# A block-scheduled transformer kernel: the first layer's normalisations and two quaternion sums, done otherwise

## What is computed

```
xn = layernorm(x)                                    # n0
a  = linear attention of xn: elu(q)+1, elu(k)+1, kv = k^T v, num / (den + 1e-6)
y  = layernorm(xn + a) * g1 + b1                     # n1 (division by den: "at")
f  = y + (silu(y Wg + bg) * (y Wu + bu)) Wd + bd     # H0 = 341 hidden
x  = x + layernorm(f) * g2 + b2                      # n2
       + sum over 8 experts e of (silu(xn Wg_e) * (xn Wu_e)) Wd_e
xn = layernorm(x)                                    # n3
for l in 4 layers:                                   # on z = xn
    z = z + filter(hamilton(hamilton(Q(q), Q(k)), Q(v))) @ pw + pb   # q,k,v of layernorm(z): "A"
    z = z + gelu(layernorm(z) @ fw + fb) @ mw + mb                   # "C"
out = x + z + top-2 of 8 experts of xn
```

## Time and profile before

| | |
|---|---|
| median of 3 runs | 1518.19 us (1517.88, 1518.19, 1524.01) |
| the profiled execution | 1522.51 us |
| its span, first to last instruction | 1520.7 us |
| mean granted TensorE clock | 0.978 of full speed |
| TensorE, VectorE, ScalarE, GpSimd busy | 92%, 82%, 69%, 24% of the span |
| TensorE weight loads | 65% |
| memory traffic | 185.59 MB read, 43.86 MB written |

### The profile page before, as it was taken

How to read it: one execution, slowest core, us unless ns; L and a number is a source line. 1 busy time by engine, 2 the same in 40 slices (tenths; PEclk the granted TensorE clock), 3 DMA queues, 4 the chain that set the end, 5 groups by cost and what they waited for, 6 DMA issues and landing times.

```text
span 1520.7 us, 20946 instructions
## 1 busy us (share of the span) xinstructions
PE 1404.2 (92%) x6198; PEld 994.6 (65%) x6198; DVE 1253.9 (82%) x1575; ACT 1046.8 (69%) x2413; POOL 361.5 (24%) x251
## 2 busy tenths in 40 slices
PE   6999998999999999899998899999889999999876
PEld 4767765666666666566655667656667787777653
DVE  3443467876999989999959897999899998999995
ACT  6556557666886777766887767777767686776552
POOL 0001202310131412111131410130524343543410
PEclk9999999999999999999999899999999999999989
DMA  7754455244545554534263335455546465655262
GB/s 268 264 210 150 148 176 193 70 130 138 187 144 154 165 174 138 188 116 120 96 220 119 103 106 159 127 153 163 161 148 211 129 204 176 199 169 155 68 177 83
DMA packets 111244, 238.03 MB, mean 157 GB/s; under 512 B 13207, under 2 KB 52844, under 8 KB 109644
## 3 DMA queue, kind: packets, MB, share of 16 engines
q1 hardware_dynamic: 106588, 227.31, 48.2%
q0 software_dynamic: 4544, 9.38, 1.8%
HBM read 185.59 MB, written 43.86 MB: 151 GB/s over the span
## 4 chain that ended last, share of the span: by engine, by line
PE 37%; issue 24%; DVE 16%; ACT 10%; POOL 9%; DMA 3%; SPq 0%; POOLq 0%; ACTq 0%; DVEq 0%
PE bank L1353 7%; PE bank L1341 6%; PE bank L1343 6%; PE bank L1342 6%; POOL RSTD L1016 4%; POOL ytok L1031 4%; PE bank L1530 3%; ACT ROWS L856 2%; DVE SH L1207 2%; DVE AM L1075 2%; DVE TA L1071 2%; PE bank L1448 2%; ACT ROWS L869 2%; DVE AM L1079 1%; PE bank L1442 1%
## 5 line engine op out<-in xcount | busy, mean ns | idle before, releaser
L1016 POOL TENSOR_TENSOR RSTD<-SS,power_half 128x4 f32<-128x4 f32 x96 | 156.8, 1633 | 835.3 <-ACT ROWS L856 835.2
L1353 PE MATMUL bank<-SH,WD 128*128 128x512 f32 x512 | 262.8, 595 | 2.1 <-DMA WD<-in_w_d 1.6
L1341 PE MATMUL bank<-NH,GU 128*128 128x512 f32 x512 | 246.4, 481 | 0.5 <-DVE SH L1207 0.5
L1207 DVE TENSOR_TENSOR SH<-SH,bank 128x512 f32<-128x512 f32 x256 | 172.5, 682 | 88.0 <-ACT SH L844 48.8
L1071 DVE TENSOR_TENSOR TA<-QKV 128x2048 f32<-128x2048 f32 x96 | 219.6, 2287 | 1.3
L1343 PE MATMUL bank<-NL,GU 128*128 128x512 f32 x512 | 202.3, 395 | 0.0
L1342 PE MATMUL bank<-NH,GU 128*128 128x512 f32 x512 | 202.2, 395 | 0.0
L844 ACT ACTIVATE SH<-bank 128x512 f32<-128x512 f32 x256 | 153.4, 605 | 63.8 <-PE bank L1343 61.8
L1031 POOL DMA_INDIRECT ytok<-YS,XR x78 | 118.1, 1514 | 152.2 <-ACT YS L1004 138.1
L1075 DVE TENSOR_TENSOR AM<-AM,TA 128x1024 f32<-128x1024 f32 x128 | 153.2, 1217 | 0.5
L869 ACT ACTIVATE ROWS<-bank,RSTD 128x128 f32<-128x128 f32 x384 | 109.9, 373 | 56.5 <-POOL RSTD L1016 48.6
(11 more groups left out here) (234 smaller groups left out, 2858.1 us busy)
## 6 DMA issues: line engine op xcount, KB each, us to landing
GU<-halves SPq DMA_DIRECT2D x112, 512.0 KB, 4.4
QKV<-QKV SPq DMA_DIRECT2D x32, 720.0 KB
GU<-in_w_gu SPq DMA_DIRECT2D x39, 512.0 KB
xg<-in_c_fill SPq DMA_DIRECT2D x8, 2080.0 KB
WD<-in_w_d SPq DMA_DIRECT2D x128, 128.0 KB
FC<-ready_w SPq DMA_DIRECT2D x32, 512.0 KB
WQ<-ready_w SPq DMA_DIRECT2D x32, 384.0 KB
WD<-in_w_d SPq DMA_DIRECT2D x39, 256.0 KB
```

The lines of the kernel that those rows point to most:

```text
L1016: pool.tensor_tensor(RSTD[:], SS[:], (power_one if k[0] == "at" else power_half)[:], ALU.pow).then_inc(power_done, 1)
L1207: dve.tensor_tensor(SH[:, g % 4, :], SH[:, g % 4, :], banks[2 + g % 2][:], ALU.mult).then_inc(h_ready, 1)
L1341: pe.matmul(out, w_hi, x_hi, start=True, stop=False)
L1353: pe.matmul(banks[4][:], WD1[:, slot, :], SH[:, g % 4, :], start=first, stop=last).then_inc(down_done, 1)
```

## The change

Two parts of the program change, and with them the plan.

1. n0 to n3 are done as A and C are: TensorE transposes, VectorE sums the rows and makes SHIFT, ScalarE squares with it as bias. Nothing downstream takes the mean out there, so there is one more step, `offset`: after `power`, VectorE makes OFFSET = -SUMS/128 x RSTD, and ScalarE scales with Identity, bias OFFSET and scale RSTD. "at", A and C scale as before.
2. The last four single-slice sums of the quaternion product become two sums over pairs of slices; the second operand of each is read with a negative step (slices 2, 0 and 3, 1), for which `pair` learns to run backwards. `HAM` is 11 in place of 13.
3. The planned steps follow this, and every number in `TUNE` is another.

```diff
-HAM, FOLD = 13, 2
+HAM, FOLD = 11, 2
...
-                     "mlp_add", "mult", "split", "route", "table", "centre"),
+                     "mlp_add", "mult", "split", "route", "table", "centre", "offset"),
...
-    "early": 169.23,
-    "norm0": (-117.36, -300.1),
-    "keys": (153.9, 106.13),
+    "early": 96.43,
+    "norm0": (-125.46, -33.96),
+    "keys": (-264.35, -414.22),
...
-    "late": 189.14,
-    "pace": 1.09,
-    "prep": (-605.23, -390.98, 38.11, -347.49),
+    "late": 446.57,
+    "pace": 2.51,
+    "prep": (-329.52, 606.46, -124.49, 268.98),
...
-            if kind in ("A", "C"):
-                step("centre", k, urgency, [(PE, 0.44, ("LN",), gives), (DVE, 0.72), (ACT_, 1.37)], after)
-            else:
-                step("centre", k, urgency, [(PE, 0.89, ("LN",), gives), (ACT_, 1.37)], after)
+            step("centre", k, urgency, [(PE, 0.44, ("LN",), gives), (DVE, 0.79), (ACT_, 1.37)], after)
             step("power", k, urgency, [(POOL, 1.5)], [("centre", k, ACT_)])
-            step("scale", k, urgency, [(ACT_, 2.0 if kind == "n3" else 1.0, ("YF",) if kind == "n3" else ())], [("power", k, POOL, 0.06)])
+            ready = [("power", k, POOL, 0.06)]
+            if kind not in ("A", "C"):
+                step("offset", k, urgency, [(DVE, 0.1)], [("power", k, POOL, 0.1)])
+                ready = [("offset", k, DVE, 0.15)]
+            step("scale", k, urgency, [(ACT_, 2.0 if kind == "n3" else 1.0, ("YF",) if kind == "n3" else ())], ready)
...
-    token_means = [x for x in scalings if x[0] in ("A", "C")]
+    token_means = [x for x in scalings if x[0] != "at"]
...
-                if k in mean_no:
-                    act.wait_ge(shift_set, mean_no[k])
+                act.wait_ge(shift_set, mean_no[k])
...
+                if k[0] in ("n0", "n1", "n2", "n3"):
+                    act.wait_ge(offset_set, upto("offset", k))
                 for i in range(GROUPS):
-                    ins = act.activation(dst[:, i, 0:P], LNB[:, i * P:(i + 1) * P], ACT.Copy, scale=RSTD[:, i:i + 1])
+                    if k[0] in ("at", "A", "C"):
+                        ins = act.activation(dst[:, i, 0:P], LNB[:, i * P:(i + 1) * P], ACT.Copy, scale=RSTD[:, i:i + 1])
+                    else:
+                        ins = act.activation(dst[:, i, 0:P], LNB[:, i * P:(i + 1) * P], ACT.Identity, bias=OFFSET[:, i:i + 1],
+                                             scale=RSTD[:, i:i + 1])
...
         def pair(ap, a, b):
+            if a > b:
+                return ap[:, a:None if b == 0 else b - 1:b - a, :]
             return ap[:, a:b + 1:b - a, :]
...
-                    5: ((2, 3), (0, 1), ADD), 6: ((0, 1), (2, 3), SUB)}
+                    5: ((2, 3), (0, 1), ADD), 6: ((0, 1), (2, 3), SUB),
+                    8: ((1, 3), (2, 0), ADD), 9: ((0, 2), (3, 1), SUB)}
...
-            elif i < 12:
-                dve.wait_ge(ham, base + 8)
-                d, s, op = ((3, 0, ADD), (2, 1, SUB), (1, 2, ADD), (0, 3, SUB))[i - 8]
-                ins = dve.tensor_tensor(AM[:, d, :], AM[:, d, :], TA[:, s, :], op)
             else:
-                dve.wait_ge(ham, base + 12)
+                dve.wait_ge(ham, base + 10)
...
+            elif name == "offset":
+                dve.wait_ge(power_done, upto("power", k))
+                dve.wait_ge(rows_scaled, upto("power", k) - 1)
+                dve.scalar_tensor_tensor(OFFSET[:], SUMS[:], -1.0 / P, RSTD[:], ALU.mult, ALU.mult).then_inc(offset_set, 1)
...
-                        if k in mean_no:
-                            mm = pe.transpose(LNB[:, i * P:(i + 1) * P], src[:, i * P:(i + 1) * P], ident[:])
-                        else:
-                            mm = pe.matmul(LNB[:, i * P:(i + 1) * P], src[:, i * P:(i + 1) * P], centre[:], start=True, stop=True)
+                        mm = pe.transpose(LNB[:, i * P:(i + 1) * P], src[:, i * P:(i + 1) * P], ident[:])
```

More of the change, by code:

```diff
@@ L145, in run @@
                 spare.remove(min(spare))
-            elif name == "ham" and key[2] == 12:
+            elif name == "ham" and key[2] == HAM - 1:
                 spare.append((at + length + 0.2, self.half[key[0:2]]))
@@ L161 @@
 TUNE = {
-    "early": 169.23,
-    "norm0": (-117.36, -300.1),
-    "keys": (153.9, 106.13),
[L165 to L176, removed]
-    "late": 189.14,
-    "pace": 1.09,
-    "prep": (-605.23, -390.98, 38.11, -347.49),
+    "early": 96.43,
+    "norm0": (-125.46, -33.96),
+    "keys": (-264.35, -414.22),
+    "kv_sum": 10.07,
+    "query": (75.18, -842.28),
+    "attn": (37.84, -213.99),
+    "norm1": (-325.66, 130.32),
+    "ffn2": (112.18, -398.42),
+    "norm2": (436.81, -400.09),
+    "route": (-147.96, 161.64),
+    "norm3": (-539.34, -168.94),
+    "start": (19.69, -8.13),
+    "layer": -33.39,
+    "each": (129.08, 164.43, 7.76, -363.31, 70.0, 158.85, -393.03, -4.03, -111.96, 224.33, -155.01, 123.2, 49.89, -176.86, 135.18, -371.38, -316.27, 16.88, 211.37, 37.35, -122.3, -37.79, 78.26, -18.71, -212.2, -225.41, -350.08, 248.52, -857.21, 138.92, 161.32, -3.96),
+    "tile": (-128.54, -313.85, -266.06, -6.81, 19.88, 152.73, -402.05, 142.08),
+    "late": 446.57,
+    "pace": 2.51,
+    "prep": (-329.52, 606.46, -124.49, 268.98),
 }
@@ L329, in schedule @@
                      [("ham", (t, l, i - 1), DVE, 0.0)] if i else [("cosines", key, ACT_), ("differences", key, DVE), ("roll", key, SP, 5.0)])
-            step("fold", key, u + 1.2, [(DVE, 1.86, ("XG",), ("AM",))], [("ham", (t, l, 12), DVE, 0.0)])
+            step("fold", key, u + 1.2, [(DVE, 1.86, ("XG",), ("AM",))], [("ham", (t, l, HAM - 1), DVE, 0.0)])
             step("freq", key, u + 1.3, [(PE, 0.86, ("6",))], [("fold", key, DVE)])
@@ L427, in program @@
     SS, RSTD = sb("SS", [P, GROUPS]), sb("RSTD", [P, GROUPS])
-    SUMS, SHIFT = sb("SUMS", [P, GROUPS]), sb("SHIFT", [P, GROUPS])
+    SUMS, SHIFT, OFFSET = (sb(n, [P, GROUPS]) for n in ("SUMS", "SHIFT", "OFFSET"))
     ROWS = sb("ROWS", [P, GROUPS, P])
@@ L851, in _ @@
                 act.wait_ge(power_done, n)
-                if k in mean_no:
-                    act.wait_ge(shift_set, mean_no[k])
+                act.wait_ge(shift_set, mean_no[k])
                 for i in range(GROUPS):
-                    shift = SHIFT[:, i:i + 1] if k in mean_no else root_eps[:]
-                    ins = act.activation(ROWS[:, i, :], LNB[:, i * P:(i + 1) * P], ACT.Square, bias=shift, scale=P ** -0.5,
+                    ins = act.activation(ROWS[:, i, :], LNB[:, i * P:(i + 1) * P], ACT.Square, bias=SHIFT[:, i:i + 1], scale=P ** -0.5,
                                          accum_out=SS[:, i:i + 1])
@@ L867, in _ @@
                 act.wait_ge(turned_back, n)
+                if k[0] in ("n0", "n1", "n2", "n3"):
+                    act.wait_ge(offset_set, upto("offset", k))
                 for i in range(GROUPS):
-                    ins = act.activation(dst[:, i, 0:P], LNB[:, i * P:(i + 1) * P], ACT.Copy, scale=RSTD[:, i:i + 1])
+                    if k[0] in ("at", "A", "C"):
[3 more added lines that the diff above has]
+                                             scale=RSTD[:, i:i + 1])
                     if k[0] == "n3":
-                        ins = act.activation(SEND[:, i, 0:P], LNB[:, i * P:(i + 1) * P], ACT.Copy, scale=RSTD[:, i:i + 1])
+                        ins = act.activation(SEND[:, i, 0:P], LNB[:, i * P:(i + 1) * P], ACT.Identity, bias=OFFSET[:, i:i + 1],
+                                             scale=RSTD[:, i:i + 1])
                 ins.then_inc(rows_scaled, 1)
@@ L1072, in hamilton @@
             elif i in sums:
-                dve.wait_ge(ham, base + (2 if i < 4 else 5))
+                dve.wait_ge(ham, base + (2 if i < 4 else 5 if i < 7 else 8))
                 d, s, op = sums[i]
                 ins = dve.tensor_tensor(pair(AM, *d), pair(AM, *d), pair(TA, *s), op)
-            elif i < 12:
-                dve.wait_ge(ham, base + 8)
-                d, s, op = ((3, 0, ADD), (2, 1, SUB), (1, 2, ADD), (0, 3, SUB))[i - 8]
-                ins = dve.tensor_tensor(AM[:, d, :], AM[:, d, :], TA[:, s, :], op)
             else:
-                dve.wait_ge(ham, base + 12)
+                dve.wait_ge(ham, base + 10)
                 ins = dve.tensor_tensor(TA[:], AM[:], own(QKV[:, h, 2, :, :]), ALU.mult)
```

4 lines of the change are left out of this document (2 added, 2 removed).

## The result

The changed kernel takes **1563.2 us** (median of 4 runs, 1558.7 to 1564.1), the kernel before, in the same session, 1521.0 (4 runs, 1517.9 to 1524.0). The ratio is 1.027, with an interval of 1.0244 to 1.0296: 42 us slower, where 5 us faster were predicted. It lies outside the range of 1492 to 1538.

The account below looks back on a forecast made before the run. Neither TensorE nor VectorE alone was taken as the bound (weights 0.70 and 0.30 where both are full). TensorE -12.0, VectorE +4.1 and longer rounds +3.0 gave -4.9 us, from 1518.2 to 1513 us; range 1492 to 1538.

Parts of the forecast that it names:

- ScalarE's waits for SHIFT: ScalarE's squares in 32 more normalisations wait for SHIFT: some 32 us more lost, of engine time not the bound.
- the 10 to 16 that were to show the prediction right: Sign on TensorE: its busy time was to fall by 10 to 16 us if the prediction was right.
- The order: All five engine queues reordered by the new TUNE: taken as 0, with 15 us kept on both sides.
- The round itself: Longer n0 to n3 normalisations: 0.5 us beyond what is counted, on 6 of 18 rounds, +3.0 us.
- TensorE's saving: Transposes replace centring products in 32 normalisations: 14.4 us of work saved, priced at -12.0 us.
- Rival 1: TensorE is the bound all through, its 14.4 us come whole: about 1502 us; chance 0.36 together with better orders.
- Rival 2: VectorE is the bound from 380 us on, so its added work counts: 1535 us; chance 0.17.
- theory W: Forecast for e8 that VectorE's added work sets the cost: +5 to +15 us.
- Rival 3: Bank 5, through which normalisations go one at a time, becomes the bound: 1526 to 1565 us; chance 0.10 beyond 1525.8.

Follow-up runs that it names:

- e1: Kernel before in its own queues, with only the last four quaternion sums made two large ones with a backward operand: ratio 0.997, 1521.1 us.
- e4: Work of the kernel before (centring products, four single-slice sums) in the changed kernel's queues: 1.0235 of the kernel before, 1561.1 us.
- e17: Work of the kernel before in the changed kernel's sequence of tiles and layers, interleaving found by local search: 1.0052 of the kernel before.
- e2: Kernel before in its old queues, only n0 to n3 done the new way, VectorE's new steps inserted at the old plan's times: 1.0467, 1597.4 us.
- e7: Kernel before in its own order, n0 to n3 using transposes with the mean left in, no row sums, SHIFT or OFFSET: ratio 0.9974.
- e8: Kernel before in its own order, n0 to n3 with transposes, row sums and SHIFT, but no OFFSET and Copy scalings: 1.0259, 1557.2 us.
- e16: Changed kernel's work in the kernel before's sequence of tiles and layers, interleaving found by local search: 1.0177 of the kernel before, 1544 us.
- e3: All of the new work, n0 to n3 and large sums, in the queues of the kernel before: ratio 1.0479, 1597.7 us.
- e10: Changed kernel with other urgency offsets, 319 of its 3921 steps moved over 3 places: 1.0293 of the kernel before, 1566.1 us.
- e11: Changed kernel with one urgency offset changed (attn, -256.38 for -213.99), 232 steps moved: 1.0295 of the kernel before, 1567.6 us.
- e13: Changed kernel's work in its own sequence of tiles and layers, interleaving found by local search: 1.0269 of the kernel before.
- e5: Changed kernel with each 2080 KB fill sent as pieces, one behind each expert weight load: 1.0185 of the kernel before, 0.85% under the changed kernel.
- e6: Kernel before with each 2080 KB fill sent as 8 pieces, one per visit: ratio 0.9924.
- e15: Kernel before's work in its own sequence, interleaving found by local search, plus two large backward-operand sums and fills in pieces: 1.0042 of the kernel before.

## Why the prediction was wrong

**What was right.** The prices of single operations, nearly all. The transposes take 0.60 us a group. OFFSET takes 0.155 us, with 0.17 taken. The scalings with a bias take 0.46. The 192 large sums, backward operand or not, take 1217 ns, at most 1249, as the 128 of before did: a negative step cost nothing here. e1 gained 4.6 us by the ratio, with an interval from 1 to 8; the prediction had 4.7 us of VectorE work, priced at 1.4. VectorE's busy time rose by 27.5 us (25 to 30 predicted). ScalarE's waits for SHIFT rose from 64.2 to 87.4 us (32 more predicted). TensorE's work did shrink by about 14: against e4, in the same order and at nearly the same granted clock (0.969 and 0.968), it is busy 13.0 us less. But its busy time against the kernel before fell by 1.5 us and not by the 10 to 16 that were to show the prediction right.

**The step that failed first: "*The order*", taken as 0 with 15 us either way.** Measured with the old work it was +36 us (e4). I treated the order as luck, independent of the work, and had no row for its size. The lengths that the planner was given changed with the work. By the planned lengths, from `centre` to `turn`, a round of n0 to n3 went from 0.89 + 0.2 + 1.37 + 0.2 + 1.5 + 0.06 + 1.0 + 0.2 = 5.42 us to 0.44 + 0.2 + 0.79 + 0.2 + 1.37 + 0.2 + 1.5 + 0.1 + 0.1 + 0.15 + 1.0 + 0.2 = 6.25. That was to be read from the diff: 32 x 0.83 = 27 us of longer rounds. In the plan itself, worked out with each kernel's `schedule()`, the time from the start of `centre` to the start of `turn` on TensorE went from 6.7 to 8.7 us, with 7.7 us of other TensorE steps in between in place of 5.4; the new lengths with the old TUNE give 8.4, in a plan that ends at 1619 us and not at 1483. So the planner did put more work between the two. e4's traced holds of n0 to n3 follow it, 11.05 us with the old work, against 9.19. e17 shows that 28 of the 36 us go when the queues are laid for the old work again. That it is this spreading, and not another trait of the new TUNE, that costs the 36 us is argued and not shown: no run has the new lengths with other offsets throughout and the old work.

**The step behind it: "*The round itself*", +3.0 us.** The size and the way of counting were both off. I took 1.1 us as the growth and charged the 0.5 beyond engine time to 6 rounds, on the chain's share. Measured in one and the same order, a hold of n0 to n3 grew by 1.77 us on average (9.19 to 10.96, e2), 57 us over 32 rounds; TensorE's idle time at their turns grew by 54.1 us, and the chip charged 71 us (e2). So all 32 rounds counted, and not 6. (The 2.04 us between the two kernels themselves are no measure of this: e4 has nearly all of it, with the old work.) In the changed kernel's own order the same work costs 18.5 us of idle time against e4, still six times the +3.0. I had counted the wait as ScalarE's ("engine time that is not the bound") and asked whether VectorE idles at the OFFSET; it does, by 10.1 us in 12 places, which costs little. The wait that costs is one step further: TensorE at the turn, and what stands behind it in its queue. My own working named the queue behind ScalarE and behind VectorE, and not the one behind the turn.

**TensorE's saving, -12.0 us**, was oversized: e7, the saving with no cost at all, gave 0.26%, 4 us of 14.4. Its idle time grew by 7.6 us (116.5 to 124.1). TensorE's 92% did not make it the bound; it waits for rounds. Rival 1 (1502 us) falls with it. In the changed kernel nearly all of the saving went as the clock fell, which the prediction didn't price: its granted mean fell from 0.978 to 0.969, e4, with the very work of before, was busy 1415.7 us instead of 1404.2, and the changed kernel is busy 15.0 us more than e7, which has the same work on TensorE and a granted clock of 0.979.

**Rival 2** (VectorE as the bound, 1535 us) has two of its three signs: VectorE's share of the chain rose from 16% to 18%, and TensorE's idle time grew. The third fails: VectorE is at 89% between 380 and 1064 us, not over 93%, and has more idle time than before, 280.3 us. e8 speaks against it too: theory W, VectorE's work, had 5 to 15 us there, and 39 were measured by the ratio. The rule behind it in the Trainium skill (Perfetto Trace Analysis, Identifying the Most-Contended Engine), by which VectorE at 82% and not TensorE with weight loads at 65% is the engine to relieve, gives the right sign here, but not the cause.

**Rival 3** came nearest. It named the round as what grows and gave 1526 to 1565; its signs, longer waits of POOL's RSTD (835.3 to 894.1 us) and holds over 11 us for n0 to n3 (11.23), are there. Yet the holds don't prove it, since e17 has 11.24 and is 0.5% slower than the kernel before. I gave it 0.10, since "the long holds are waits for a busy VectorE or ScalarE, which other work fills". The argument failed in the old queues, where TensorE, in order, couldn't fill a wait at its own turn. Bank 5 as such isn't full: the 104 holds make 1218 us of 1562 (32 x 11.23, 8 x 7.63, 64 x 12.46), 78%, as against 77% before. That the time of 1563 us lies at the end of its range (1526 to 1565) is in part luck, since that range had nothing for the order.

**What stays open.** The exact split between idle at the turn, room made by the planner and the lower clock in the changed kernel; the turn idle grew by 16.5 us only, and 6.2 of these at n0 to n3; the rest of the 42.5 lies at other waits (`centre`, experts, queries, `mproj`), which I can't attribute one by one. So the loss at the turn is shown for the old queues, and for the changed kernel in part. Whether a better order for the new work exists than e16's isn't excluded; six orders were run with it (the changed kernel's, e3, e10, e11, e13, e16), and none came under 1.0177.

## What to carry to other kernels

Where an engine with an in-order queue hands a tile out and takes it back, a growth of that round trip for which the queue has no room is a cost of its own: price it by rounds times growth, at the engine that waits at the return, and not by busy time. In a fixed order this gave 57 us, with 54 measured at the returns. Moving 0.45 us of work off the fullest engine is a loss if it puts two hops and nearly 2 us into the loop it must wait for. And when a planner orders the queues, read the lengths that it is given and run the old work in the new order: the order was the larger part here (36 us), and the work's own price at equal treatment was 26 to 33; the two don't add up to the 42, since the old work doesn't fit the new order nor the new work the old one.

## What the runs showed of the hardware

- A second operand read with a step of minus two slices (the elements within a slice forwards) cost VectorE nothing here: a median of 1217 ns for 128x1024 before, without such steps, and after, with them in 64 of 192.
- On ScalarE a 128x128 Identity with bias and scale columns takes 458 ns, a Copy with a scale column 373 ns.
- A small load issued shortly behind bulk copies on one queue was late: MP took 16.5 us behind two fills and three loads, against a median of 4.3 us. With the fills in eighths, one per visit, the whole kernel took 0.8% less in e5 and e6; in e15, in another order and with the sums of e1, nothing was gained.
- The granted clock is another in another order of the same work: 0.978 before, 0.968 in e4, with TensorE busy 11.5 us more for it. TensorE's idle time alone doesn't tell it: e2 has 180.7 us and 0.962, but e8 155.8 us and 0.979.
